# Three edge tables folded while the fourth comes, the diagonal's default written to memory, and TensorE loops in the first stage of a graph-attention layer

## The chip, the cores and the metric

The kernel runs on one core of a Trainium2 chip. Its time is the device time in microseconds (us) of one launch. Three runs of the kernel before gave 503.61, 492.89 and 503.67 us; the median is 503.61.

## The reference

384 nodes with 1024 features go through a layer norm, then two branches are added to them, then a second norm and an expert block. All matrices are fp32. Cut to what matters:

```python
xn = layernorm(x)                                   # (384, 1024)
q = xn @ wq.T + bq;  k = xn @ wk.T + bk;  v = xn @ wv.T + bv
q2, k2, v2 = heads(q @ wiq.T + biq), heads(k @ wik.T + bik), heads(v @ wiv.T + biv)   # 16 heads of 64
mask = full((384, 384), -inf)
mask = mask.at[src, dst].set(w[edge_type - 1])      # 12288 edges, the last of a pair counts
diag = diagonal(mask)                               # a missing diagonal becomes w[3]
mask = mask.at[i, i].set(where(isneginf(diag), w[3], diag))
attn = softmax(q2 @ k2.T * scale + mask)
x = x + (attn @ v2) @ wo.T + bo + mixer(xn)         # mixer: coeff = sum_d(fq * fk), coeff * v, @ Wo + bo
x = x + expert_ffn(layernorm(x))                    # one of 8 experts, chosen by a loss over the nodes
```

w is softplus of four edge weights. The mixer has three 1024x1024 projections and one back.

## The kernel before, in words

It is written by hand, engine by engine. Each engine's program is a fixed list, and semaphores order the lists among each other. Every 1024x1024 matrix comes in eight blocks of 128x1024, 512 KB each. A block is split in two parts of reduced precision: ScalarE writes the high part (line 554), VectorE the rest (line 927), and TensorE multiplies high by high, high by low and low by high. A `column_job` (line 1315) is that for one block: 24 matmuls of 384 columns, 16 at line 1321 and 8 at 1326. A `row_block` (line 1334) is 18 matmuls of 512 columns at line 1331.

**First stage.** 32 column jobs make q, k, v and q2 (jobs 0 to 7, 8 to 15, and so on). Weight slots and PSUM banks go round by four: job a uses slot `A_SLOTS[a % 4]` for the time a // 4 and bank `A_BANKS[a % 4]`. The fourth slot lies in tiles that are used later on: its raw weights in `mask`, its parts in `probT`; the profile shows these names for it. Jobs 0 to 23 read the normalised input xT, jobs 24 to 31 (q2) read q in T0. After them come v2 in eight row blocks, and between its halves the first k2 job.

**The edges beside it.** On VectorE each job also handles 3 of 96 columns of 128 edges: it compares keys (line 982) to find edges that a later one in the same column replaces, and writes addresses to `where` (line 989). GpSimd then scatters a column's weights to a table of 384x384 values in memory, one indirect DMA per column (line 470). Two edges of different columns can hit the same place, so scatters to one table must follow each other. There are four tables, each with a quarter of the edges and taken in turn 1, 2, 3, 0; a table's next scatter waits until its last one has landed. A later table's edges are to win. The tables begin as ABSENT (line 459). At the end GpSimd loads them to SBUF (line 479), table 0 to `mask`, the others to the three `later` regions of U.

**The mask on VectorE.** Its program has eight weight splits for the v2 stage; between the seventh and the last stands `default_diagonal`, behind the last `merge_table` three times. The diagonal is treated in table 0 alone: three comparisons (line 1007) and three predicated copies (line 1011). Each merge marks the present places of one table (line 1018) and copies them into the mask (line 1020).

**The pairs.** Then eight pairs of heads follow. Each has scores on TensorE (line 1447), six reads of scores plus mask on VectorE (line 1092), exponentials and normalising on ScalarE (lines 677, 684), a transposing trip of the probabilities through memory (VectorE 1108, SP's queue 383 and 391, ScalarE 665, VectorE 1073), the product with v2 (line 1459), and four column jobs: the next k2, and the mixer's q, k and v. The job of the mixer's q takes a PSUM bank that a score had, so TensorE waits in pair 0 until all six reads are done (`score_read`, line 1493).

Of the kernel before, what the change touches and what calls it, by code (L numbers as in the profile page):

```python
# [18 lines left out]
U32 = mybir.dt.uint32  # L19
ALU = mybir.AluOpType  # L20
# [4 lines left out]
P = 128  # L25
N = 384
D = 1024
NT = N // P
KB = D // P
# [6 lines left out]
STREAMS = 4  # L36
DEEP = CH // STREAMS
# [12 lines left out]
FIRST = 32  # L50
# [59 lines left out]
def gps_layer(nc, x, out, weights, conv, down, upT, up_b, down_b, conv_b, disc, bias_cols,  # L110
              rows, edge_weights, edge_rows, edge_cols, consts):
    with ExitStack() as ctx:
# [3 lines left out]
        def sem(name):  # L116
            return ctx.enter_context(nc.semaphore(name))
# [86 lines left out]
        row_bo = Q2[:].rearrange("p k n -> p (k n)")[:, 0:2 * D].rearrange("p (r d) -> p r d", r=2)  # L204
        k2f = U[:, NT * D:2 * NT * D]
        blank = Q2[:, 0:NT, :]
        bare = U[:, 4608:4608 + NT * P].rearrange("p (t n) -> p t n", t=NT)
        bias_rows = k2f[BIAS_ROW:BIAS_ROW + 2, 0:D]
        raw_down = k2f[:, D:D + KB * R].rearrange("p (k r) -> p k r", k=KB)
        raw_up = k2f[:, D + 512:D + 512 + KB * R].rearrange("p (k r) -> p k r", k=KB)  # L210
# [50 lines left out]
        where_ready = sem("where_ready")  # L261
        blanked = sem("blanked")
        first_mask_in = sem("first_mask_in")
        diag_step = sem("diag_step")
        scattered = [sem(f"scattered{g}") for g in range(STREAMS)]
        table_in = [sem(f"table_in{g}") for g in range(1, STREAMS)]
        mask_step = sem("mask_step")
# [171 lines left out]
        def _(pool):  # L439
# [22 lines left out]
            pool.wait_ge(key_calc, 1)  # L462
            pool.dma_start(key_dram, erow[:, 0:P]).then_inc(key_out, 16)

            for k in range(CH):

                g = QUARTERS[k % STREAMS]
                pool.wait_ge(where_ready, k // CJ + 3)
                pool.wait_ge(scattered[g], 16 * (k // STREAMS + 1))
                pool.indirect_dma_start(  # L470
                    tables[g], bass.IndirectOffsetOnAxis(ap=where[:, k:k + 1], axis=0),
                    evalue[:, k:k + 1], None, bounds_check=N * N - 1,
                    oob_is_err=False).then_inc(scattered[g], 16)
            for g, into in enumerate([mask[:]] + later):
                pool.wait_ge(scattered[g], 16 * (DEEP + 1))
                if g == 0:

                    pool.wait_ge(lo_ready[A_SLOTS[3]], FIRST // 4 + 1)
                pool.dma_start(into, tables[g].rearrange("(t p n) o -> p t (n o)", t=NT, p=P)).then_inc(
                    table_in[g - 1] if g else first_mask_in, 16)  # L480
# [361 lines left out]
        def _(dve):  # L842
# [156 lines left out]
                                             in1=dst[0][:, j, :].bitcast(F32), op0=ALU.add,  # L999
                                             op1=ALU.subtract).then_inc(bank_free[a % 4], 1)  # L1000

            def default_diagonal():

                dve.wait_ge(first_mask_in, 16)
                dve.wait_ge(id_in, 16)
                for t in range(NT):
                    dve.scalar_tensor_tensor(out=bare[:, t, :], in0=mask[:, t, t * P:(t + 1) * P], scalar=ABSENT,
                                             in1=ident, op0=ALU.is_equal, op1=ALU.mult).then_inc(diag_step, 1)
                dve.wait_ge(diag_step, NT)
                for t in range(NT):  # L1010
                    dve.copy_predicated(mask[:, t, t * P:(t + 1) * P], bare[:, t, :].bitcast(U32),
                                        ew[:, 3:4].broadcast_to([P, P])).then_inc(diag_step, 1)
                dve.wait_ge(diag_step, 2 * NT)

            def merge_table(g):

                dve.wait_ge(table_in[g], 16)
                dve.tensor_scalar(present, later[g], ABSENT, None, ALU.not_equal).then_inc(mask_step, 1)
                dve.wait_ge(mask_step, 2 * g + 1)
                dve.copy_predicated(mask[:].rearrange("p t n -> p (t n)"),  # L1020
                                    present.bitcast(U32).rearrange("p t n -> p (t n)"),
                                    later[g].rearrange("p t n -> p (t n)")).then_inc(mask_step, 1)
                dve.wait_ge(mask_step, 2 * g + 2)

            for a in range(FIRST):
                job(a)
# [24 lines left out]
            for r in range(9):  # L1051
                if r < 8:
                    split_weights(*slot_use(r + 2))
                if r == K2_FIRST:
                    q2_lo(0)
                if r == K2_FIRST + 1:
                    k2_lo(0)
                if r == 6:
                    default_diagonal()
            for g in range(STREAMS - 1):  # L1060
                merge_table(g)

            def pv_sum(j, h):
                r = slice(64 * h, 64 * h + 64)
# [240 lines left out]
        def _(pe):  # L1305
# [9 lines left out]
            def column_job(slot, use, src, bank):  # L1315

                o = PS[:, bank, 0:N]
                pe.wait_ge(hi_ready[slot], use + 1)
                for part in range(2):
                    for k in range(KB):  # L1320
                        pe.matmul(o, w_hi[slot][:, k * P:(k + 1) * P], src[part][:, k, :],  # L1321
                                  start=(k == 0 and part == 0), stop=False)
                pe.wait_ge(lo_ready[slot], use + 2)
                for k in range(KB):
                    wl = w_lo[slot][:, k * P:(k + 1) * P]
                    last = pe.matmul(o, wl, src[0][:, k, :], start=False, stop=(k == KB - 1))  # L1326
                last.then_inc(w_used[slot], 1)
# [80 lines left out]
            whole_part(1, w_hi, 1, False, False)  # L1408
            pe.wait_ge(lo_ready[A_SLOTS[1]], 2)
            whole_part(1, w_lo, 0, False, True).then_inc(w_used[A_SLOTS[1]], 1)  # L1410
            for a in range(2, FIRST):
                pe.wait_ge(bank_free[a % 4], a // 4 + 1)
                column_job(*A_USES[a], T0 if a >= 3 * KB else xT, A_BANKS[a % 4])

            for half in range(2):
                for kp in range(4):
# [246 lines left out]
```

## Time and profile before

| | |
|---|---|
| median of three runs | 503.61 us (492.89 to 503.67) |
| profiled execution, its own time | 478.61 us |
| its span, first to last instruction | 476.8 us |
| TensorE busy | 466.1 us, 98% |
| VectorE, ScalarE, GpSimd busy | 346.6, 258.5, 156.0 us |
| mean granted clock of TensorE | 0.993 |

The page of the profile gives these and the chain of work that ended last. By it 57% of the span is TensorE and 20% DMA; up to 195 us it runs through the scatters (15% and 7% for their DMAs and their issue), the mask's load and VectorE's merges, from there on through TensorE. A timeline row is: start, duration, engine, line, operation, output and input, how many, and in brackets the idle time before it with what ended it. Where neighbouring instructions are merged the duration is that of all of them.

### The profile page before, as it was taken

The numbers are of one execution on the slowest core, as the hardware profiler recorded it, in microseconds if no ns is written. First come the engines' busy times: TensorE is split into PE (matmuls) and PEld (weight loads), VectorE is DVE, ScalarE is ACT, GpSimd is POOL, SyncE is SP. The second block draws the span as 40 slices with busy tenths as digits, with TensorE's granted clock in tenths as the row PEclk, the third lists the DMA queues.
The fourth block names the chain that finished last, engine by engine and source line by source line (L and its number), as shares of the span: only waits on it lengthen the run. The fifth ranks groups of instructions, "written<-read, shape, count | busy, mean of one in ns | idle before, by whom it ended". The sixth has DMA issues, their size and how long they took to land.

```text
span 476.8 us, 7326 instructions
## 1 busy us (share of the span) xinstructions
PE 466.1 (98%) x2521; PEld 432.9 (91%) x2521; DVE 346.6 (73%) x796; ACT 258.5 (54%) x423; POOL 156.0 (33%) x176
## 2 busy tenths in 40 slices
PE   7999999999999999799999999999999999999996
PEld 5999999999999888699999999999998888888885
DVE  6968976677626237778889897898876994587394
ACT  3734533333324344668888788888875362163170
POOL 3136767767767762000210103022026000040200
PEclk9999999999999999799999999999999999999999
DMA  7876776566554446376676667577669854210463
GB/s 249 314 212 222 232 216 167 177 182 177 156 148 151 132 126 250 131 226 202 207 257 191 221 197 217 202 228 253 188 224 346 297 184 164 88 35 11 138 261 132
DMA packets 39049, 91.92 MB, mean 193 GB/s; under 512 B 7410, under 2 KB 20306, under 8 KB 38884
## 3 DMA queue, kind: packets, MB, share of 16 engines
q1 hardware_dynamic: 33604, 83.15, 54.2%
q0 software_dynamic: 4832, 7.45, 4.7%
q10 hardware_dynamic: 576, 0.85, 0.6%
q8 instruction: 20, 0.33, 0.3%
q14 instruction: 17, 0.14, 0.1%
HBM read 77.96 MB, written 13.47 MB: 192 GB/s over the span
## 4 chain that ended last, share of the span: by engine, by line
PE 57%; DMA 20%; issue 10%; POOL 7%; DVE 4%; POOLq 0%; ACT 0%; DVEq 0%; SPq 0%
PE PS L1331 21%; PE PS L1321 18%; DMA table<-evalue,where 15%; PE PS L1326 9%; POOL table L470 7%; PE PS L1459 4%; PE PS L1447 3%; PE PS L1583 2%; DMA mask<-table 1%; DMA U<-x 1%; DMA raw<-weights 1%; DMA key_dram<-V 1%; DMA U<-key_dram 1%; PE PS L1587 1%; DVE mask L1020 1%
## 5 line engine op out<-in xcount | busy, mean ns | idle before, releaser
L927 DVE TENSOR_TENSOR w_lo<-raw,w_hi 128x1024 fp32r<-128x1024 f32 x86 | 105.0, 1232 | 44.1 <-ACT w_hi L554 43.7
L554 ACT ACTIVATE w_hi<-raw 128x1024 fp32r<-128x1024 f32 x87 | 90.9, 1054 | 72.4 <-PE PS L1331 47.0
L470 POOL DMA_INDIRECT table<-evalue,where x96 | 104.4, 1087 | 48.0 <-issue 24.4
L1321 PE MATMUL PS<-xT_hi,w_hi 128*128 128x384 f32 x320 | 63.3, 339 | 3.3 <-DVE smax L1092 3.3
L1321 PE MATMUL PS<-xT_lo,w_hi 128*128 128x384 f32 x320 | 63.1, 339 | 0.0
L1326 PE MATMUL PS<-xT_hi,w_lo 128*128 128x384 f32 x320 | 62.0, 334 | 0.0
L1321 PEld LDWEIGHTS PS<-xT_hi,w_hi 128*128 128x128 f32 x320 | 57.1, 191 | 3.6 <-DVE smax L1092 3.6
L1321 PEld LDWEIGHTS PS<-xT_lo,w_hi 128*128 128x128 f32 x320 | 57.2, 191 | 0.0
L1326 PEld LDWEIGHTS PS<-xT_hi,w_lo 128*128 128x128 f32 x320 | 56.3, 188 | 0.0
L1331 PE MATMUL PS<-w_hi,T_hi 128*128 128x512 f32 x144 | 40.1, 391 | 0.0
L1331 PE MATMUL PS<-w_hi,T_lo 128*128 128x512 f32 x144 | 39.8, 389 | 0.0
L982 DVE SCALAR_TENSOR_TENSOR U<-U,V,cst 128x128 f32<-128x128 f32 x96 | 33.6, 350 | 8.0 <-DMA U<-key_dram 5.6
L1331 PE MATMUL PS<-w_lo,T_hi 128*128 128x512 f32 x144 | 37.8, 389 | 0.0
L616 ACT ACTIVATE T_hi<-PS,bias 128x384 fp32r<-128x384 f32 x24 | 13.8, 576 | 39.5 <-PE PS L1326 39.5
L502 POOL CAST vs<-V 128x384 fp32r<-128x384 f32 x8 | 5.0, 629 | 83.9 <-PE PS L1459 75.9
L1331 PEld LDWEIGHTS PS<-w_hi,T_lo 128*128 128x128 f32 x144 | 27.0, 188 | 5.7
L1331 PEld LDWEIGHTS PS<-w_lo,T_hi 128*128 128x128 f32 x144 | 27.0, 188 | 5.6
L1331 PEld LDWEIGHTS PS<-w_hi,T_hi 128*128 128x128 f32 x144 | 27.0, 188 | 5.2
L677 ACT ACTIVATE U<-U,nmax 128x384 f32<-128x384 f32 x48 | 28.9, 605 | 5.1 <-DVE nmax L1096 5.1
L1108 DVE STREAM_TRANSPOSE U<-U 128x384 f32<-128x384 f32 x48 | 24.1, 552 | 9.7 <-DMA turn<-U 9.7
L684 ACT ACTIVATE U<-U,rsum 128x384 f32<-128x384 f32 x48 | 25.8, 604 | 0.0
L997 DVE SCALAR_TENSOR_TENSOR T_lo<-PS,bias,T_hi 128x384 fp32r<-128x384 f32 x24 | 14.7, 615 | 14.9 <-ACT T_hi L616 14.9
(247 smaller groups left out, 810.9 us busy)
## 6 DMA issues: line engine op xcount, KB each, us to landing
raw<-weights SPq DMA_DIRECT2D x84, 512.0 KB, 4.5
turn<-U SPq DMA_DIRECT2D x16, 576.0 KB, 4.2
U<-turn SPq DMA_DIRECT2D x64, 144.0 KB, 2.9
U<-key_dram SPq DMA_DIRECT2D x32, 192.0 KB, 4.2
mask<-weights SPq DMA_DIRECT2D x9, 512.0 KB, 4.8
table<-Q POOLq DMA_DIRECT2D x4, 576.0 KB, 10.7
V<-conv SPq DMA_DIRECT2D x4, 512.0 KB, 5.3
U<-table POOLq DMA_DIRECT2D x3, 576.0 KB, 7.8
```

The source lines that it names most:

```text
L470: pool.indirect_dma_start(tables[g], bass.IndirectOffsetOnAxis(ap=where[:, k:k + 1], axis=0), evalue[:, k:k + 1], None, bounds_check=N * N ...
L554: act.activation(w_hi[slot][:], raw[slot][:], ACT.Copy).then_inc(hi_ready[slot], 1)
L677: act.activation(prob[:, h, t, :], prob[:, h, t, :], ACT.Exp, bias=nmax[:, h, t:t + 1], scale=SCALE, accum_out=ssum[:, h, t:t + 1]).then_i ...
L684: act.activation(prob[:, h, t, :], prob[:, h, t, :], ACT.Copy, scale=rsum[:, h, t:t + 1]).then_inc(prob_ready, 1)
L927: dve.tensor_tensor(w_lo[slot][:], raw[slot][:], w_hi[slot][:].bitcast(F32), ALU.subtract).then_inc(lo_ready[slot], 1)
L982: dve.scalar_tensor_tensor(out=key_junk, in0=key_row[:, s, c * P:(c + 1) * P], scalar=ekey[:, ch0 + c:ch0 + c + 1], in1=tri, op0=ALU.is_eq ...
L997: dve.scalar_tensor_tensor(out=dst[1][:, j, :], in0=PS[:, A_BANKS[a % 4], 0:N], scalar=bias[:, a:a + 1], in1=dst[0][:, j, :].bitcast(F32), ...
L1108: dve.transpose(blocks.rearrange("p (c m t i) -> p t m c i", c=NQ, m=NT, t=NT)[:, t], prob[:, h, t, :].rearrange("p (m c i) -> p m c i", m ...
L1321: pe.matmul(o, w_hi[slot][:, k * P:(k + 1) * P], src[part][:, k, :], start=(k == 0 and part == 0), stop=False)
L1326: last = pe.matmul(o, wl, src[0][:, k, :], start=False, stop=(k == KB - 1))
L1331: return pe.matmul(bank, src[part][:, 2 * kp + k2, t * P:(t + 1) * P], weights_in[slot][:, k2 * HALF:(k2 + 1) * HALF], start=start, stop=stop)
L1459: last = pe.matmul(PS[:, 7, 0:N], vs[:, m, h, :], probT[part][:, m, :], start=(m == 0 and part == 0), stop=(m == NT - 1 and part == 1))
```

## The change

Four edits. (1) A DMA on GpSimd's queue writes w[3] to the 384 diagonal places of table 0 in memory, after its blank and ahead of all scatters; an edge on the diagonal overwrites it. `default_diagonal` goes. (2) GpSimd loads the tables in the order 1, 2, 3, 0. (3) VectorE folds table 2 into table 1, then table 3, and copies the outcome into table 0's mask at the end. The first fold stands where the diagonal stood. (4) TensorE's jobs 4 to 31 become two loops over rounds of four jobs, five rounds that read xT and two that read T0; the waits take their values from a register.

```diff
+            pool.wait_ge(prep, 7)
+            pool.wait_ge(scattered[0], 16)
+            pool.dma_start(tables[0][::N + 1, :].rearrange("(t p) o -> p (t o)", p=P),
+                           ew[:, 3:4].broadcast_to([P, NT]), allow_slow_non_contiguous=True).then_inc(scattered[0], 16)
             for k in range(CH):
                 g = QUARTERS[k % STREAMS]
                 pool.wait_ge(where_ready, k // CJ + 3)
-                pool.wait_ge(scattered[g], 16 * (k // STREAMS + 1))
+                pool.wait_ge(scattered[g], 16 * (k // STREAMS + 1 + (g == 0)))
...
-            for g, into in enumerate([mask[:]] + later):
-                pool.wait_ge(scattered[g], 16 * (DEEP + 1))
+            for g, into in [(1, later[0]), (2, later[1]), (3, later[2]), (0, mask[:])]:
+                pool.wait_ge(scattered[g], 16 * (DEEP + 1 + (g == 0)))
...
-            def default_diagonal():
...
-            def merge_table(g):
-
+            def fold_table(g):
+
+                dve.wait_ge(table_in[0], 16)
                 dve.wait_ge(table_in[g], 16)
                 dve.tensor_scalar(present, later[g], ABSENT, None, ALU.not_equal).then_inc(mask_step, 1)
-                dve.wait_ge(mask_step, 2 * g + 1)
+                dve.wait_ge(mask_step, 2 * g - 1)
+                dve.copy_predicated(later[0].rearrange("p t n -> p (t n)"),
+                                    present.bitcast(U32).rearrange("p t n -> p (t n)"),
+                                    later[g].rearrange("p t n -> p (t n)")).then_inc(mask_step, 1)
+                dve.wait_ge(mask_step, 2 * g)
+
+            def merge_tables():
+
+                dve.tensor_scalar(present, later[0], ABSENT, None, ALU.not_equal).then_inc(mask_step, 1)
+                dve.wait_ge(first_mask_in, 16)
+                dve.wait_ge(mask_step, 5)
                 dve.copy_predicated(mask[:].rearrange("p t n -> p (t n)"),
                                     present.bitcast(U32).rearrange("p t n -> p (t n)"),
-                                    later[g].rearrange("p t n -> p (t n)")).then_inc(mask_step, 1)
+                                    later[0].rearrange("p t n -> p (t n)")).then_inc(mask_step, 1)
...
                 if r == 6:
-                    default_diagonal()
-            for g in range(STREAMS - 1):
-                merge_table(g)
+                    fold_table(1)
+            fold_table(2)
+            merge_tables()
...
-            for a in range(2, FIRST):
-                pe.wait_ge(bank_free[a % 4], a // 4 + 1)
-                column_job(*A_USES[a], T0 if a >= 3 * KB else xT, A_BANKS[a % 4])
+            for a in (2, 3):
+                pe.wait_ge(bank_free[a], 1)
+                column_job(*A_USES[a], xT, A_BANKS[a])
+
+            for src, begin, end in ((xT, 1, 3 * KB // 4), (T0, 3 * KB // 4, FIRST // 4)):
+                with pe.Fori(0, end - begin) as i:
+                    for s in range(4):
+                        pe.wait_ge(bank_free[s], i + (begin + 1))
+                        column_job(A_SLOTS[s], i + begin, src, A_BANKS[s])
```

VectorE between the last split of the v2 stage's first part and the first score read, before (w_lo is a weight split, U holds the tables and the marks):

```order
L927 TENSOR_TENSOR w_lo<-raw,w_hi 128x1024 [waits hi_ready2]
L1007 SCALAR_TENSOR_TENSOR U<-mask,cst 128x128 [waits id_in,first_mask_in]
L1007 SCALAR_TENSOR_TENSOR U<-mask,cst 128x128 x2
L1011 COPY_PREDICATED mask<-U,ew 128x128 [waits diag_step]
L1011 COPY_PREDICATED mask<-U,ew 128x128 x2
L927 TENSOR_TENSOR w_lo<-raw,w_hi 128x1024 [waits hi_ready0,diag_step]
L1018 TENSOR_SCALAR U<-U 128x1152 [waits table_in1]
L1020 COPY_PREDICATED mask<-U 128x1152 [waits mask_step]
L1018 TENSOR_SCALAR U<-U 128x1152 [waits table_in2,mask_step]
L1020 COPY_PREDICATED mask<-U 128x1152 [waits mask_step]
L1018 TENSOR_SCALAR U<-U 128x1152 [waits table_in3,mask_step]
L1020 COPY_PREDICATED mask<-U 128x1152 [waits mask_step]
```

and now, where `table_in1` to `table_in3` stand for tables 1 to 3 and `first_mask_in` for table 0:

```order
L930 TENSOR_TENSOR w_lo<-raw,w_hi 128x1024 [waits hi_ready2]
L1009 TENSOR_SCALAR U<-U 128x1152 [waits table_in2,table_in1]
L1011 COPY_PREDICATED U<-U 128x1152 [waits mask_step]
L930 TENSOR_TENSOR w_lo<-raw,w_hi 128x1024 [waits hi_ready0,mask_step]
L1009 TENSOR_SCALAR U<-U 128x1152 [waits table_in3,table_in1]
L1011 COPY_PREDICATED U<-U 128x1152 [waits mask_step]
L1018 TENSOR_SCALAR U<-U 128x1152 [waits mask_step]
L1021 COPY_PREDICATED mask<-U 128x1152 [waits mask_step,first_mask_in]
```

The wait for table 0 moved from ahead of all this work to the last instruction; six small instructions are gone.

TensorE at the start of the first loop, as it is now (before, the same rows without the first two and without the register step follow each other for all 28 jobs):

```order
L1417 UNCONDITIONAL_BRANCH
L1417 ISA
L1322 MATMUL PS<-xT_hi,w_hi 128x384 [waits hi_ready0,bank_free0]
L1322 MATMUL PS<-xT_hi,w_hi 128x384 x7
L1322 MATMUL PS<-xT_lo,w_hi 128x384 x8
L1324 REGISTER_ALU
L1327 MATMUL PS<-xT_hi,w_lo 128x384 [waits lo_ready0]
L1327 MATMUL PS<-xT_hi,w_lo 128x384 x7
```

and at its end:

```order
L1327 MATMUL PS<-xT_hi,probT_lo 128x384 x7
L1417 REGISTER_ALU
L1417 COMPARE_AND_BRANCH
L1417 UNCONDITIONAL_BRANCH
L1417 ISA
```

The matmuls and their waits are the same; a few control instructions came in per round.

## Rows read from the trace of the kernel before

**Rows 1.** The page: TensorE's busy time and instructions, matmuls and weight loads.
```profile
PE 466.1 (98%) x2521; PEld 432.9 (91%) x2521; DVE 346.6 (73%) x796; ACT 258.5 (54%) x423; POOL 156.0 (33%) x176
```
**Rows 2.** Waits of TensorE: who waited for whom, us, times, longest.
```profile
PE PS L1321 <- DVE smax L1092: 3.3, 1, 3.3
```
**Rows 3.** Timeline of TensorE around 195 us.
```profile
190.33 1.55 PE L1326 MATMUL PS<-T_hi,w_lo 128*128 128x384 f32 x8
195.20 2.93 PE L1321 MATMUL PS<-xT_hi,w_hi 128*128 128x384 f32 x8 [3.31 <-DVE smax L1092]
...
201.97 1.55 PE L1321 MATMUL PS<-xT_hi,w_hi 128*128 128x384 f32 x8
```
**Rows 4.** Windows: width, busy by engine, granted clock, DMA share, GB/s.
```profile
195.20:200.70 5.50, 5.50 (x17) 5.50 (x18) 4.93 (x10) 5.50 (x15) 0.00 (x0) 0.51 0.51 167
```
**Rows 5.** Timeline of GpSimd: last scatters and the table loads.
```profile
167.23 1.23 POOL L470 DMA_INDIRECT table<-evalue,where  x1 [0.30 <-DMA table<-evalue,where]
...
170.03 0.97 POOL L470 DMA_INDIRECT table<-evalue,where  x1 [0.30 <-issue]
171.31 1.33 POOL L470 DMA_INDIRECT table<-evalue,where  x1 [0.30 <-issue]
175.38 0.80 POOL L479 DMA_DIRECT2D mask<-table  x1 [2.74 <-DMA table<-evalue,where]
176.17 2.31 POOL L479 DMA_DIRECT2D U<-table  x3
```
**Rows 6.** DMA: busy tenths per us of 160 to 200; issues, median us to landing.
```profile
DMA  5900390039202830569999999880000000000597
...
table<-Q POOLq DMA_DIRECT2D x4, 576.0 KB, 10.7
U<-table POOLq DMA_DIRECT2D x3, 576.0 KB, 7.8
table<-evalue,where POOLq DMA_INDIRECT x96, 3.8
...
mask<-table POOLq DMA_DIRECT2D x1, 576.0 KB, 5.9
```
**Rows 7.** Timeline of VectorE from the last split to the merged mask.
```profile
174.69 1.23 DVE L927 TENSOR_TENSOR w_lo<-raw,w_hi 128x1024 fp32r<-128x1024 f32 x1 [2.37 <-ACT w_hi L554]
181.33 0.70 DVE L1007 SCALAR_TENSOR_TENSOR U<-mask,cst 128x128 f32<-128x128 f32 x3 [5.41 <-DMA mask<-table]
182.06 0.71 DVE L1011 COPY_PREDICATED mask<-U,ew 128x128 f32<-128x128 uint32 x3
...
183.94 0.75 DVE L1018 TENSOR_SCALAR U<-U 128x1152 f32<-128x1152 f32 x1
184.73 1.55 DVE L1020 COPY_PREDICATED mask<-U 128x1152 f32<-128x1152 uint32 x1
...
188.91 1.42 DVE L1018 TENSOR_SCALAR U<-U 128x1152 f32<-128x1152 f32 x1
190.37 1.55 DVE L1020 COPY_PREDICATED mask<-U 128x1152 f32<-128x1152 uint32 x1
```
**Rows 8.** Timelines of SP's queue and ScalarE: the first probability block comes back.
```profile
203.65 1.77 SPq L391 DMA_DIRECT2D U<-turn  x4
...
208.92 1.15 ACT L665 ACTIVATE probT_hi<-U 128x1152 fp32r<-128x1152 f32 x1
```
**Rows 9.** Timelines of GpSimd, VectorE and TensorE, up to 35 us.
```profile
10.71 3.04 POOL L459 DMA_DIRECT2D table<-Q  x4 [6.88 <-DMA raw<-weights]
...
34.70 0.97 POOL L470 DMA_INDIRECT table<-evalue,where  x1 [0.30 <-issue]
...
28.15 0.35 DVE L982 SCALAR_TENSOR_TENSOR U<-U,V,cst 128x128 f32<-128x128 f32 x1 [3.71 <-DMA U<-key_dram]
...
30.69 1.66 PE L1326 MATMUL PS<-xT_hi,probT_lo 128*128 128x384 f32 x8 [0.70 <-DVE probT_lo L927]
```
**Rows 10.** The page: TensorE's code queue (packets, MB, share of 16 engines).
```profile
q8 instruction: 20, 0.33, 0.3%
```

More of the change, by code:

```diff
@@ L206, in gps_layer @@
         blank = Q2[:, 0:NT, :]
-        bare = U[:, 4608:4608 + NT * P].rearrange("p (t n) -> p t n", t=NT)
         bias_rows = k2f[BIAS_ROW:BIAS_ROW + 2, 0:D]
@@ L263, in gps_layer @@
         first_mask_in = sem("first_mask_in")
-        diag_step = sem("diag_step")
         scattered = [sem(f"scattered{g}") for g in range(STREAMS)]
@@ L1000, in job @@
                                              op1=ALU.subtract).then_inc(bank_free[a % 4], 1)
-            def default_diagonal():
[L1004 to L1013, printed above, removed]
-            def merge_table(g):
+            def fold_table(g):
+                dve.wait_ge(table_in[0], 16)
                 dve.wait_ge(table_in[g], 16)
                 dve.tensor_scalar(present, later[g], ABSENT, None, ALU.not_equal).then_inc(mask_step, 1)
-                dve.wait_ge(mask_step, 2 * g + 1)
+                dve.wait_ge(mask_step, 2 * g - 1)
[7 more added lines that the diff above has]
+                dve.wait_ge(mask_step, 5)
                 dve.copy_predicated(mask[:].rearrange("p t n -> p (t n)"),
                                     present.bitcast(U32).rearrange("p t n -> p (t n)"),
-                                    later[g].rearrange("p t n -> p (t n)")).then_inc(mask_step, 1)
-                dve.wait_ge(mask_step, 2 * g + 2)
+                                    later[0].rearrange("p t n -> p (t n)")).then_inc(mask_step, 1)
+                dve.wait_ge(mask_step, 6)
             for a in range(FIRST):
```

## The prediction

> **What bounds the kernel now.** I read the engine totals first. TensorE is busy for 98% of the span, so only TensorE's own work and its few gaps can carry time [rows 1]. Next the waits of TensorE: the longest is 3.3 us for the last of six mask reads on VectorE (the softmax inputs of pair 0) [rows 2]. The timeline there shows the ending k2 job at 190.33 with 1.55 us, then nothing until 195.20 [rows 3]; the job ended at 190.33 + 1.55 = 191.9. The eight matmuls behind the gap take 2.93 us, later ones of the same shape 1.55. The granted clock says why: from 195.20 to 200.70 it is 0.51, which is 1.2 GHz of 2.4, after 3.3 us without matmuls [rows 4]. At half clock 5.5 us do the work of 2.75. So this place costs 3.3 + 2.7 = 6.0 us, and that is all the change can win here while TensorE has the rest of its work.
>
> Third, what ends that wait. It is a chain beside TensorE: the scatters, the table loads, then the merges on VectorE. The last four scatters (tables 1, 2, 3, 0) start between 167.23 and 171.31, the mask's load is issued at 175.38, the other three behind it [rows 5]. A scatter lands 3.8 us after its issue, the first load after 5.9, the other three after 7.8 as the median; the DMA share is near zero at 171 and again at 175 us and nine tenths from 178 on [rows 6]. VectorE has been free since 174.69 + 1.23 = 175.9 and waits 5.41 us for the mask; then 0.70 + 0.71 for the diagonal, 1.23 for a weight split, three comparisons and three predicated copies (1.55 the first, the third comparison 1.42), up to 191.9; then six reads, after which TensorE starts at 195.2, so 3.3 us for them [rows 3, 7].
>
> **The change, part by part.** *Table loads in the order 1, 2, 3, 0.* With 3.8 us to land, the last scatters of tables 1, 2 and 3 (167.23, one between, 170.03) are in at about 171.0, 172.5 and 173.8. GpSimd's queue issues its last scatter until 171.31 + 1.33 = 172.6. So the loads go out at 172.9, 173.7 and 174.5 (0.8 each, as now), and the mask's at 175.4 as now. The first two go to DMA engines that are nearly idle, so I take 5.9 us for table 2: in at 179.6. Table 3: 180.4 to 182.3 with 5.9 or 7.8. Table 0, now last, 7.8: 183.2 (5.9 would give 181.3).
>
> *VectorE.* Six diagonal instructions go, 0.70 + 0.71 = 1.4 us, which were on the chain. The large ones stay three comparisons and three copies, 0.75 + 1.55 = 2.3 a pair by the quickest. New order: fold of table 2 from 179.6 to 181.9; the weight split queued behind it to 183.1; fold of table 3 to 185.4; comparison to 186.2; copy into the mask to 187.8, for which table 0 (183.2) is in. The mask is ready at 187.8, not at 191.9: 4.1 us earlier. Bounds: loads 1.9 later and one comparison at 1.42 give 190.4 (1.5 us earlier); table 2 landing as fast as a scatter, in 3.8, gives 185.7 (6.2 earlier). Six reads in 3.3 us end at 191.1, and TensorE asks at 191.9. The wait goes, and with it the low clock: **-6.0 us**, less what the next parts cost. At the late bound 190.4 the reads end at 193.7, a wait of 1.8. The low clock set in somewhere in the 3.3 us gap; whether one of 1.8 would escape it is open. "TensorE: Matmul & The Clock Gate" of the Trainium skill, Part 1, says that the gate looks at times of its own, independent of the kernel. By that rule a short gap might meet the low clock or not from run to run, and this part would lie between -1.5 (dip kept) and -4.2 (dip gone) for this bound.
>
> *What is late next.* The pair's first probability block goes VectorE, memory, back, ScalarE, VectorE, TensorE. The reload is issued from 203.65 on, four pieces in 1.77 us, about 3 us to land, so in at 208; ScalarE takes it at 208.92 without waiting [rows 8]. TensorE's need moves 6.0 us earlier, the block only 4.1 (VectorE's reads): 1.9 us against 0.9 of slack. I charge 0.3, bounds 0 and 1.0. The later pairs show no TensorE wait.
>
> *The diagonal written to memory.* One DMA of 384 single elements on GpSimd's queue. It waits for VectorE's scaled edge weights, which come before any scatter's address, and for table 0's blank, the last of four issued by 13.75 and 10.7 us to land, thus about 24 us. Its issue is bounded by the 0.76 of a blank (also 384 rows), and it is out before the first address exists, which the key read of 28.15 has to precede. Table 0's first scatter comes at 34.70: more than the 10.7 us, the longest landing shown, so that scatter does not wait. What it can disturb: the key read that VectorE waits for until 28.15 (3.71 idle), and behind that the weight split that TensorE waits 0.70 for at 30.69 [rows 9]. A delay there reaches TensorE one for one. Below: nothing. Above: 3.8 us, the landing of a whole scatter. The elements equal three scatters, which elsewhere pass at 1.3 us each beside weight loads; spread over 16 engines they hardly occupy one. I charge 0.3. "DMA: Bandwidth & Descriptors" of the Trainium skill, in its closing tables, says that a strided last dimension becomes one descriptor per element; it gives no other sum here.
>
> *The loops.* Jobs 4 to 23 become five rounds and 24 to 31 two, 96 matmuls and their weight loads a round. The matmuls are the same. Added are a branch and a register step per round, five jumps back in all. TensorE works without a gap in this stage, and since the mask wait is gone, a bubble here would count fully. No row of this kernel shows a jump. Below: 0, since the sequencer may be ahead; above: if each jump had to fetch code anew, a page of code. The 20 pages of TensorE's code queue took 0.3% of 16 engines' span, 0.003 x 476.8 x 16 / 20 = 1.1 us each in transfer [rows 10], and a DMA as small as a scatter needs 3.8 to land: 5 x 3.8 = 19. Nearest is the case of a jump within code that is there: a round holds 192 matmuls and loads of some 5,042, or 0.76 of a page. I charge 0.3. "Advanced Engine Details and Errata" of the Trainium skill (Control Flow Timing) has about 108 ns for a compare-and-branch; five make 0.5 as an estimate by that page, and the sum would be 0.2 worse. The four fewer pages of code are worth nothing: 0.3% of the engines' time in all.
>
> *Sum.* -6.0 + 0.3 + 0.3 + 0.3 = -5.1. The profiled execution took 478.6 us (span 476.8 and 1.8 around it), so 473.5 in a profile. The median shown is 503.6, 25 us above it, and the three runs lie 10.8 apart. The trace doesn't contain these 25. If they lengthen the scatters, the mask wait is longer and 4 to 6 us still come off; if they are in TensorE, less comes off. I take the difference: 503.6 - 5.1 = **498.5 us**.
>
> **Rivals.** A measurement of this kernel tells 2%, about 10 us, from no change.
> (1) *Forecast*: wait and low clock go, 496 to 501. Chance 0.50.
> (2) *The mask is hardly the limit in unprofiled runs, or part of the wait and the low clock stay.* With the late bound and the dip kept, 478.6 - 1.5 + 0.9 is no change; so 501 to 505. For: 25 us unexplained. Against: the wait is the longest there is. Chance 0.22.
> (3) *The loops stall TensorE.* Place: the five jumps back. A jump refetches code, 3.8 us each, 19 in all; against -6.0 that is +13. If every gap also brings a dip of 2.7 as the one at 195, up to 5 x 2.7 = 13.5 more: 517 to 530. Break-even is 6.0 / 5 = 1.2 us a jump; slower by 2% needs 16 / 5 = 3.2. "Runtime: NRT & Kernel Launch" of the Trainium skill (Instruction fetch mechanics) states the rule: a jump to a target outside the two fetched pages stalls for a DMA, and full unrolling is preferred. For: a round of 0.76 page can begin in one page and end in the next. Against: the code came in by single pages spaced like the work without one gap in TensorE, so the sequencer is ahead, and what is queued covers a jump. Chance 0.08.
> (4) *The change comes out at a lower level than the median shown.* One of three runs took 492.9; with -5.1 that is 487.8. If a shorter chain makes such runs the rule, the gain passes 2%. For: 10.8 us between runs of one program is more than the whole place costs in the profile, so something else than the rows decides it, and a chain with slack would be less exposed. Against: nothing in the trace shows it. Chance 0.17.
> (5) A higher level unseen so far, 505 to 515, 0.03.
>
> The range takes (1), (2) and (4): **487 to 505**, leaving out (3), (5) and the ends. Faster by over 2% (below 493.5): (4) and a tail of (1), 0.22. Slower (above 513.7): (3) and part of (5), 0.10. Within: 0.68.
>
> **What would show it.** Loads of tables 1 to 3 issued from 172.9 on and the mask's last at 175.4; the last copy ending near 187.8; TensorE's wait for the mask read under 1 us, and no stretch of granted clock 0.5 near 195; TensorE's matmuls of jobs 4 to 31 without gaps. Wrong if gaps stand every 96 matmuls and more than 20 code pages arrive; if the first key read lands later than 28.1; or if the low clock comes all the same.

## The result: the change saves nothing that the median shows

In the first comparison, 22 launches (executions) of each kernel, the change has a median of **495.10 us** (491.45 to 503.33), the kernel before 494.74 (490.04 to 503.67): 0.1% apart. The comparison itself gives a ratio of 1.0186, 95% interval 1.0119 to 1.0253, which leaves open whether the change is slower by 2%; it goes by the launches within 1.5% of a kernel's fastest, but of these 16 and 14 launches the medians are 493.84 and 492.58, 0.3% apart, so I don't rest anything on it. The profiled launch of the change took 501.14 us. On four chips used later both kernels run some 20 us faster, and three comparisons there give the change 0.9988 [0.9950, 1.0026], 1.0013 [0.9977, 1.0049] and 0.9991 [0.9955, 1.0027] of before: no change. The forecast was 498.5. The measured 495.10 lies in the range of 487 to 505, but the gain of 5.1 did not come: the median of before had itself come down, from 503.61 over three launches to 494.74 over 22.

The page of the change's profile, first comparison (answers to [rows 1, 10]; PEclk is the granted clock in tenths, 40 slices of 12.5 us):

```profile
span 499.3 us, 7352 instructions
PE 476.3 (95%) x2521; PEld 435.3 (87%) x2521; DVE 343.5 (69%) x790; ACT 257.3 (52%) x423; POOL 153.4 (31%) x177
PEclk9999967997999899999999999999999999999999
q8 instruction: 16, 0.26, 0.2%
```

TensorE has the same 2521 matmuls, is busy for 10 us more than before and has 23 us outside its matmuls, against 10.7. The low clock is not near 195 us (slice 15 of 0 to 39) but in slices 5, 6, 9 and 13: about 62 to 87, 112 to 125 and 162 to 175 us. Four pages of code fewer arrive, as the shorter program has it.

Its waits of TensorE, the answer to [rows 2] (who waited for whom, us, times, longest):

```profile
PE PS L1322 <- issue: 9.2, 15, 1.4
PE PS L1327 <- issue: 5.6, 8, 1.3
PE PS L1369 <- DVE w_lo L886: 1.6, 1, 1.6
...
PE PS L1454 <- ACT U L751: 0.4, 1, 0.4
PE PS L1466 <- DVE probT_lo L1074: 0.2, 1, 0.2
```

The wait for the mask read is gone. In its place stand 14.8 us in 23 gaps put down to "issue": no engine and no transfer that the profile shows was waited for. The timeline of TensorE in the same launch shows how they look (start, duration, instruction, idle time before):

```profile
60.87 1.55 PE L1322 MATMUL PS<-xT_hi,probT_hi 128*128 128x384 f32 x8
62.25 1.47 PE L1322 MATMUL PS<-xT_lo,probT_hi 128*128 128x384 f32 x6
64.36 0.51 PE L1322 MATMUL PS<-xT_lo,probT_hi 128*128 128x384 f32 x2 [0.63 <-issue]
65.80 0.42 PE L1327 MATMUL PS<-xT_hi,probT_lo 128*128 128x384 f32 x1 [0.93 <-issue]
67.22 0.48 PE L1327 MATMUL PS<-xT_hi,probT_lo 128*128 128x384 f32 x1 [0.99 <-issue]
...
76.43 0.48 PE L1322 MATMUL PS<-xT_hi,w_hi 128*128 128x384 f32 x1 [1.41 <-issue]
77.13 2.20 PE L1322 MATMUL PS<-xT_hi,w_hi 128*128 128x384 f32 x5 [0.23 <-issue]
```

Eight matmuls in a row normally start 1.39 us apart from the next eight, 0.17 each. Here single ones start 0.7 or a multiple of it apart. Windows over the three stretches follow, then the first two of them in another launch of the change, the second of its three repeats below, where TensorE has no gap (width; busy by PE, PEld, DVE, ACT, POOL; granted clock; DMA share; GB/s):

```profile
60.00:80.00 20.00, 12.10 (x41) 9.01 (x41) 3.73 (x12) 2.98 (x5) 12.59 (x13) 0.67 0.24 66
...
110.00:125.00 15.00, 10.77 (x41) 8.72 (x40) 5.22 (x18) 4.53 (x6) 7.44 (x8) 0.77 0.23 75
...
150.00:166.00 16.00, 12.95 (x58) 10.69 (x58) 3.54 (x12) 3.63 (x5) 10.68 (x11) 0.89 0.09 25
```

```profile
60.00:80.00 20.00, 20.00 (x117) 20.00 (x116) 13.86 (x42) 7.66 (x10) 14.53 (x14) 1.00 0.69 190
...
110.00:125.00 15.00, 15.00 (x89) 15.00 (x88) 10.46 (x34) 5.47 (x8) 11.97 (x10) 1.00 0.64 189
```

117 matmuls in 20 us against 41. The low clock (1.2 of 2.4 GHz) came behind each stretch's first gaps, from 66.8 for 13.7 us, from 118.0 for 6.8 and from 162.3 for 3.4, 23.9 us in all. From job 0 to the first v2 column the launch takes 162.5 us where the profiled launch of before took 134.9, 27.6 more. Of these 14.8 are the gaps, and the other 12.8 are matmuls that took longer: in the 23.9 us TensorE is busy for 16.2, so the half clock accounts for 8.1 at most, and the rest are matmuls that stand alone, 0.33 to 0.5 us each where those in a row come 0.17 apart. The eight score pairs (first score to first output block) take 155.65 us against 160.48, and what stands behind them 130.6 both times. The gain in the pairs has the forecast's sign, but this launch can't show that it is the fold's: TensorE came 27 us late, and the mask, complete at 212.15, was ready 1.9 us before the first read of a score at 214.00.

### The profile page after: what moved, and what is told of

It reads as the page before. It is cut to its first block, busy times and chain, and to the rows that moved or that the text cites. A ratio compares the mean times of both kernels' runs of the same rounds, so it can differ in the third digit from the quotient of the medians.

```text
span 499.3 us, 7352 instructions
## 1 busy us (share of the span) xinstructions
PE 476.3 (95%) x2521; PEld 435.3 (87%) x2521; DVE 343.5 (69%) x790; ACT 257.3 (52%) x423; POOL 153.4 (31%) x177
## 4 chain that ended last, share of the span: by engine, by line
PE 89%; issue 3%; DVE 3%; DMA 3%; ACT 0%; SPq 0%; DVEq 0%
PE PS L1322 35%; PE PS L1332 26%; PE PS L1327 18%; PE PS L1466 4%; PE PS L1454 3%; PE PS L1590 1%; DMA U<-x 1%; DMA key_dram<-V 1%; PE PS L1310 1%; DMA U<-key_dram 1%; PE PS L1594 1%; DVE U L1298 1%; PE PS L1574 1%; DVE probT_lo L1074 0%; DVE stats L857 0%
## 5 line engine op out<-in xcount | busy, mean ns | idle before, releaser
L473 POOL DMA_INDIRECT table<-evalue,where x96 | 100.9, 1051 | 59.9 <-issue 29.7
L1322 PE MATMUL PS<-xT_hi,w_hi 128*128 128x384 f32 x320 | 65.2, 342 | 3.3 <-issue 3.2
L1327 PE MATMUL PS<-xT_hi,w_lo 128*128 128x384 f32 x320 | 63.5, 339 | 0.6 <-issue 0.6
```

Source lines behind the costliest of these rows:

```text
L473: pool.indirect_dma_start(tables[g], bass.IndirectOffsetOnAxis(ap=where[:, k:k + 1], axis=0), evalue[:, k:k + 1], None, bounds_check=N * N ...
```

## The experiments

On each of the four later chips the kernels ran interleaved with the kernel before. Times are medians with lowest and highest, then the number of launches, the ratio to before and its 95% interval. The expectations speak of theory A, that the loops starve TensorE of instructions, and theory B, that the slow stretches come to any kernel at random; from the delay experiment on also of theory C, that the end of the mask's chain and TensorE's need of it nearly coincide, so that a launch has the wait with its low clock or neither.

**The change and the kernel before again, elsewhere.** No edit.

> The whole change once more. Theory A: slow stretches again at the same places of the loops, 490 to 503 us. Theory B: slow stretches at other places, their number differing from launch to launch.

Measured: 474.95 (473.33 to 477.67, 12 launches), ratio 0.9988 [0.9950, 1.0026]. No slow stretch came, which neither theory had expected.

> The kernel before once more, for another profile of it. Theory A: TensorE has no idle time by issue, as in the profile shown, and the 490 to 503 us have another cause. Theory B: it has 10 to 20 us by issue, in stretches with steps of about 0.7 us, at places that don't repeat, and the span is 12 to 25 us above the 476.8 shown. Ratio 1.00 in both.

Measured: 474.18 (472.54 to 478.39, 12), ratio 1.0008 [0.9967, 1.0049]; its profiled launch, span 471.3, has no mask wait although nothing was edited. What differs from the first profile is one time stamp. Timelines of GpSimd and VectorE of this launch, answers to [rows 5, 7]:

```profile
169.88 0.97 POOL L470 DMA_INDIRECT table<-evalue,where  x1 [0.30 <-issue]
172.35 0.80 POOL L479 DMA_DIRECT2D mask<-table  x1 [1.50 <-DMA table<-evalue,where]
...
177.61 0.69 DVE L1007 SCALAR_TENSOR_TENSOR U<-mask,cst 128x128 f32<-128x128 f32 x3 [1.85 <-DMA mask<-table]
...
185.89 1.56 DVE L1020 COPY_PREDICATED mask<-U 128x1152 f32<-128x1152 uint32 x1
```

The mask's load goes out at 172.35, not 175.38, and the last copy ends at 187.45, not 191.92. Ninety-six scatters stand ahead of it. Their end moves by more than these 3 us: in six profiled launches with the old load order the mask's load goes out at 167.79, 171.46, 171.53, 172.35, 175.38 and 175.66. TensorE waits for the mask in the last two and in no other.

**The table edits alone, the loops alone.** The first is the change with TensorE's code of before, the second the kernel before with the change's loops. The edit of the first:

```
-            for a in (2, 3): ... (both Fori loops)
+            for a in range(2, FIRST):
+                pe.wait_ge(bank_free[a % 4], a // 4 + 1)
+                column_job(*A_USES[a], T0 if a >= 3 * KB else xT, A_BANKS[a % 4])
```

> The change without the loops: diagonal in memory, loads in the order 1, 2, 3, 0, the fold. Theory A: no slow stretch, no wait for the mask read, no low clock near 195 us, 472 to 475 us in the profile, ratio 0.985 to 0.99. Theory B: slow stretches as in before, TensorE late at the mask either way, so the fold wins little: ratio 0.99 to 1.00.

Measured: 473.33 (472.17 to 474.78, 12), ratio 0.9945 [0.9909, 0.9981], and no wait for the mask.

> The kernel before with TensorE's two loops and nothing else. Theory A (the loops starve TensorE of instructions, in stretches of 10 to 15 us in which matmuls come at steps of about 0.7 us): such stretches lie in jobs 4 to 31, TensorE's idle time by issue is 10 to 20 us, ratio to before 1.01 to 1.03. Theory B (the stretches come to any kernel at random, and the profile shown of before was a launch without one): ratio 0.995 to 1.005, since the loops cost nothing by themselves. Both: with a stretch in the first stage TensorE reaches the mask late and its wait there is gone.

Measured: 476.31 (474.29 to 479.84, 12), ratio 1.0011 [0.9974, 1.0048]. Its profiled launch has the mask wait and a low clock, and no gap in jobs 4 to 31: from job 4 to the first v2 column 116.5 us with loops (32.32 to 148.80), 116.5 without (before again, 32.03 to 148.51). Timeline of GpSimd and waits of TensorE:

```profile
175.66 0.81 POOL L479 DMA_DIRECT2D mask<-table  x1 [2.89 <-DMA table<-evalue,where]
```

```profile
PE PS L1321 <- DVE smax L1092: 2.9, 1, 2.9
```

The forecast's mechanism is there, the loops' stall is not.

**What the mask's lateness is worth.** In both orders four GpSimd fills of an unused tile (4.42 us in all) are put between the last scatter and the table loads. They wait until the last scatter has landed, so all four tables are complete when the first load goes out.

```
+            pool.wait_ge(scattered[QUARTERS[-1]], 16 * (DEEP + 1))   # + 2 in the new order
+            for n in range(4):
+                pool.memset(present, 0.0).then_inc(delayed, 1)
+                pool.wait_ge(delayed, n + 1)
             for g, into in ...
```

> The kernel before, with GpSimd filling an unused region four times (about 1 us each) between the last scatter and the table loads, so that the mask comes about 4 us later. Theory C (the mask chain and TensorE's 191.8 us arrive together, so a launch either has the wait with a low clock behind it or has neither): now every launch waits 4 to 8 us, with a low clock: 481 to 485 us, +7 to +11 over the lower half of the launches before, ratio about 1.015 to 1.02. Rival (the wait is not what separates the launches at 474 and at 479 us): the two groups stay, both up by 4 at most.

Measured, old order: 478.65 (477.75 to 480.27, 4), ratio 1.0100 [1.0040, 1.0161]. That is less than the 481 to 485 expected, but the two groups of times are gone as theory C has it: the mean granted clock of all four launches is 0.992 to 0.996.

> The same 4 us in the kernel with the change's table edits and without its loops. Theory C: the fold gives back 3 to 4 us here in every launch, so TensorE's wait is under 4 us, 477 to 481 us, 3 to 6 less than the kernel before with the same delay. Rival (the fold wins little since VectorE's work is the same): at most 2 less.

Measured, table edits: 480.80 (479.28 to 480.95, 4), ratio 1.0134 [1.0076, 1.0192]. I had expected the new order to be the faster one here, and it is the slower. Timelines of GpSimd, VectorE and TensorE, first old order, then new:

```profile
177.47 0.81 POOL L484 DMA_DIRECT2D mask<-table  x1 [0.30 <-POOL U L477]
...
182.18 0.69 DVE L1012 SCALAR_TENSOR_TENSOR U<-mask,cst 128x128 f32<-128x128 f32 x3 [5.74 <-DMA mask<-table]
...
191.20 1.54 DVE L1025 COPY_PREDICATED mask<-U 128x1152 f32<-128x1152 uint32 x1
...
196.03 2.44 PE L1326 MATMUL PS<-xT_hi,w_hi 128*128 128x384 f32 x8 [3.62 <-DVE smax L1097]
```

```profile
177.50 2.34 POOL L487 DMA_DIRECT2D U<-table  x3 [0.41 <-POOL U L480]
179.82 0.77 POOL L487 DMA_DIRECT2D mask<-table  x1
...
184.88 0.76 DVE L1014 TENSOR_SCALAR U<-U 128x1152 f32<-128x1152 f32 x1 [8.51 <-DMA U<-table]
...
192.59 1.43 DVE L1026 COPY_PREDICATED mask<-U 128x1152 f32<-128x1152 uint32 x1
...
197.31 2.93 PE L1327 MATMUL PS<-xT_hi,w_hi 128*128 128x384 f32 x8 [4.97 <-DVE smax L1098]
```

With all tables ready at the same time, the old order starts its diagonal on one landed table 4.7 us after the first load; the new one needs two and starts after 7.4. From there VectorE needs 9.1 us to the complete mask where the old order needs 10.6, so 1.4 of the 2.7 come back and 1.3 stay. So the folding order gains only when tables 1 to 3 are complete ahead of the last: what it buys is above all the earlier loads. TensorE's wait and half clock follow the mask's end (192.7: wait 3.6, 194.0: wait 5.0), so lateness of the mask does cost time; what is not there in most launches is the lateness.

**The diagonal's default alone.** The edge weights are written by DMA, VectorE's six instructions go, orders stay.

```
+            pool.dma_start(tables[0][::N + 1, :]..., ew[:, 3:4].broadcast_to([P, NT]), ...)
...
-                if r == 6:
-                    default_diagonal()
```

> The kernel before with the diagonal written to memory and without VectorE's six diagonal instructions; loads and merges in the old order. The mask comes 1.4 us earlier, which takes the wait of 3.3 to 1.9 in a late launch and away in an early one: ratio 0.996 to 1.000, fewer launches at 478 and more. If the 384 single elements delay the key read (VectorE's first comparison after 28.2 us, TensorE's wait at 30 us above 1.0): 0 to 1 us slower than before.

Measured: 475.72 (472.90 to 478.11, 10), ratio 1.0030 [0.9986, 1.0073], no gain; TensorE waits 0.6 for the low part behind the key read, before waits 0.58 and 0.70. The upper group of launches is still there, five of ten at 477.0 to 478.1, where before's own on this chip has a median of 478.9, which would fit 1.4 us less in late launches; ten launches are too few to show it. Its profiled launch is an early one. There the mask is complete 15.8 us after the first load, and 15.5 in the last profile of before: the weight split behind them waits for ScalarE and starts at 178.67 without them and at 178.70 with them, so they cost nothing there.

**Repeats, to tell the median's shift from chance.** The change, the table edits and before again:

> The whole change a third time. Theory B (slow stretches of TensorE's issue belong to the launch and the place, not to the kernel): none, 473 to 478 us, ratio 0.995 to 1.003, unless the kernel before is at 490 and more too. Theory A (the loops bring them): stretches in some launches, a spread to 490 us and more while the kernel before stays at 474.

Measured: 474.83 (473.76 to 476.74, 10), 1.0013 [0.9977, 1.0049].

> The kernel before, for a third profile of it. Theory B: where this place runs launches at 474 to 479 us, TensorE has no idle time by issue; where it runs them at 490 and more, it has 10 to 20 us of it in stretches with steps of 0.7 us, as the change had. Theory A: before never shows such a stretch, wherever it runs.

Measured: 473.84 (472.44 to 479.07, 10), 1.0001 [0.9945, 1.0058]. Timeline of GpSimd in its profiled launch, the earliest load of all:

```profile
167.79 0.80 POOL L479 DMA_DIRECT2D mask<-table  x1 [1.45 <-DMA table<-evalue,where]
```

> The table edits without the loops once more. Theory C: all launches between 472 and 475 us where before has two groups at 474 and 479: ratio 0.990 to 0.998. If the 1.5 us between its median and that of the whole change were chance, it is 474.5 or more here.

Measured: 473.58 (471.92 to 479.31, 10), 0.9960 [0.9911, 1.0009]. Seven of the ten launches lie between 471.9 and 474.5 as expected, the others at 475.77, 477.08 and 479.31.

> The kernel before, once more. Theory B: at a place with launches of 490 us and more its profile has TensorE idle by issue in steps of 0.7 us, 10 to 27 us in all; at a place with 474 to 479 none. Theory A: never.

Measured: 473.82 (472.35 to 478.30, 10), 0.9984 [0.9941, 1.0026].

> The whole change, beside it. Theory B: like the kernel before at the same place, within 1%. Theory A: 15 to 25 us more than before wherever stretches occur. At a quiet place both say 474 to 477 us, ratio 0.998 to 1.003.

Measured: 475.01 (472.79 to 476.51, 10), 0.9991 [0.9955, 1.0027].

**Other loops.** With the table edits, one loop of two rounds of eight jobs (jobs 4 to 19), the rest written out:

```
+            with pe.Fori(1, 5, 2) as i:
+                for s in range(8):
+                    pe.wait_ge(bank_free[s % 4], i + (1 + s // 4))
+                    column_job(A_SLOTS[s % 4], i + s // 4, xT, A_BANKS[s % 4])
```

> The change with one loop of two rounds of eight jobs (jobs 4 to 19, 384 matmuls and weight loads a round, 1.5 code pages) and the rest written out. If a jump over more than the pages at hand fetches code anew: one or two more packets in TensorE's code queue than its code needs, and a gap of 1 to 4 us at 100 us, if nothing that is queued covers it. If TensorE keeps more than two pages, or the queued matmuls cover the fetch: no gap, ratio 0.995 to 1.002 as for the change.

Measured: 472.66 (471.87 to 474.31, 10), 0.9947 [0.9908, 0.9985].

> The one loop of eight jobs once more, with one jump back instead of five. If jumps cost about 0.3 us each: 472 to 473.5 us again, 1.5 to 2 below the change. If the place decides instead, it moves with the tables-only kernel to within 0.5 us of it.

The same kernel on another chip: 472.69 (471.69 to 474.23, 10), 0.9958 [0.9919, 0.9997]. Its round is 1.5 pages of code by the instruction count. The page's code queue and TensorE's timeline around the jump back at 64.95, in the first of the two:

```profile
q8 instruction: 18, 0.29, 0.3%
```

```profile
63.57 1.55 PE L1327 MATMUL PS<-xT_hi,probT_lo 128*128 128x384 f32 x8
64.95 1.37 PE L1322 MATMUL PS<-xT_hi,w_hi 128*128 128x384 f32 x7
```

Eighteen packets, two fewer than before, and no gap (1.38 us from one eight to the next): no packet came beyond the program's own length, so what the jump goes back to was not fetched again. Then the change with only its first loop (jobs 4 to 23, four jumps) and only its second (24 to 31, one jump):

```
-            for src, begin, end in ((xT, 1, 3 * KB // 4), (T0, 3 * KB // 4, FIRST // 4)):
+            for src, begin, end in ((xT, 1, 3 * KB // 4),):
...
+            for a in range(24, FIRST):
+                pe.wait_ge(bank_free[a % 4], a // 4 + 1)
+                column_job(*A_USES[a], T0, A_BANKS[a % 4])
```

> The change with its first loop (five rounds of four jobs, four jumps back) and jobs 24 to 31 written out. If each jump costs about 0.3 us, or the first loop all of it: 1.2 to 1.5 over the table edits without loops (473.4), so 474.6 to 475. If the loops cost nothing by themselves: 473.0 to 473.8.

Measured: 473.67 (472.05 to 475.73, 10), 0.9950 [0.9910, 0.9991].

> The change with its second loop alone (two rounds, one jump back), jobs 4 to 23 written out. By jumps: 473.5 to 474. If it is the second loop that costs 1.5 us, which stands where the scatters are latest: 474.8 or more.

Measured: 473.44 (472.38 to 474.12, 10), 0.9949 [0.9910, 0.9988].

## Why the prediction was wrong, step by step

**The step that failed: "I take the difference: 503.6 - 5.1".** It takes the wait of the profiled launch for one that every launch has. Not every launch has it. Over the four chips there are 116 launches of before that ran beside the others, with their mean granted clock:

| kernel | launches | clock under 0.998 | their median | median of the others | mean of all |
|---|---|---|---|---|---|
| before | 116 | 41 | 478.56 | 473.64 | 475.54 |
| the change | 32 | 0 | | 474.83 | 474.95 |
| table edits, no loop | 22 | 1 | 479.31 | 473.37 | 473.71 |
| table edits, one of the two loops | 20 | 0 | | 473.57 | 473.61 |
| table edits, loop of eight jobs | 20 | 0 | | 472.66 | 472.83 |
| loops alone | 12 | 2 | 478.65 | 476.13 | 476.29 |
| the diagonal's default alone | 10 | 3 | 477.49 | 473.96 | 475.63 |

The 32 launches of before in the repeats above split alike, 8 and 24. The profile that I read is of the kind of the 41 (478.61, clock 0.993). In these the launch takes 478.56 - 473.64 = 4.9 us more, and no launch of the change is of that kind. In the other 75 the clock shows no loss; the profiled ones among such launches have the mask in time, so there is nothing to win, and the median launch is one of them. What is left there is what the change adds, 474.83 - 473.64 = 1.2 us. The median stays, and the mean falls by 0.6. The table edits without loops bring the mean down by 1.8, and 41 of 116 launches times 4.9 make 1.7. The delay experiment shows the same from the other side: with the loads held back by 4.4 us, all four launches of before lie at 478 to 480.

That 495.10 lies in the range is luck. The sum was laid on 503.61, the median of three launches, of which two are the slowest of the 22; the level of this place, 494.74, made up for the gain that is missing.

**-6.0 for the wait and the low clock: right for such a launch, a little large.** In the second repeat of the change the mask came as forecast. Timelines of GpSimd and VectorE:

```profile
171.54 1.32 POOL L473 DMA_INDIRECT table<-evalue,where  x1 [0.30 <-issue]
172.85 2.36 POOL L482 DMA_DIRECT2D U<-table  x3
175.80 0.76 POOL L482 DMA_DIRECT2D mask<-table  x1 [0.58 <-DMA table<-evalue,where]
...
179.87 0.76 DVE L1009 TENSOR_SCALAR U<-U 128x1152 f32<-128x1152 f32 x1 [3.73 <-DMA U<-table]
...
186.62 1.58 DVE L1021 COPY_PREDICATED mask<-U 128x1152 f32<-128x1152 uint32 x1
```

Loads from 172.85 (forecast 172.9), the mask's at 175.80 (175.4), first fold 179.87 (179.6), mask ready at 188.2 (187.8), TensorE without a wait at 191.94. The launch's pairs take 155.77 against 160.48, -4.7 where -6.0 + 0.3 was summed, and its span is 472.4 against 476.8, -4.4 against -5.1. In the two other repeats the loads began earlier still, at 169.77 and 169.19.

**+0.3 for what is late next: mis-sized.** Two of TensorE's waits in that launch:

```profile
PE PS L1454 <- ACT U L751: 0.6, 1, 0.6
PE PS L1466 <- DVE probT_lo L1074: 0.2, 1, 0.2
```

I named the probability block (0.2); the larger part, 0.6, is ScalarE's copy of the value bias (L751) that stands behind that block's split on ScalarE. Pair 1 lasts 21.8 us, 1.1 longer than in the profile of before, at my upper bound of 1.0; in the three profiled launches of before without the mask wait it lasts 21.0 to 21.2. It doesn't come in each launch: the launch of eight-job loops has neither wait.

**+0.3 for the diagonal: nothing.** In the first comparison, timelines of GpSimd, VectorE and TensorE, answers to [rows 9]:

```profile
24.23 0.77 POOL L465 DMA_DIRECT2D table<-ew  x1 [4.17 <-DMA table<-Q]
29.91 1.24 POOL L473 DMA_INDIRECT table<-evalue,where  x1 [4.91 <-DVE where L992]
...
27.70 0.35 DVE L985 SCALAR_TENSOR_TENSOR U<-U,V,cst 128x128 f32<-128x128 f32 x1 [3.46 <-DMA U<-key_dram]
...
30.24 1.67 PE L1327 MATMUL PS<-xT_hi,probT_lo 128*128 128x384 f32 x8 [0.45 <-DVE probT_lo L930]
```

Issued at 24.23 for 0.77 (forecast 24 and 0.76), and the key read is in at 27.7, not later than 28.15. In two repeats of the change it is in at 28.22 and 28.36, past the 28.1 that I had named as a sign of being wrong; but with loops alone, where nothing is written to the diagonal, it is in at 28.28, and in the old order with the delay at 28.68, so that sign tells nothing. The 1.4 us taken off for the six instructions of `default_diagonal` hold for loads as late as in the first profile; with early ones they are not on the chain, as the experiment with the diagonal alone shows.

**+0.3 for the loops: too small in the median, and not where the rival put it.** Both loops together stand at 474.83 against 473.37 without, 1.5 us, in launches without a low clock; the loops alone at 476.13 against 473.64, 2.5 us; and each of the three medians of the change (474.95, 474.83, 475.01) is above both of the table edits (473.33, 473.58). But four jumps alone give 473.67, one alone 473.44, and two rounds of eight jobs 472.66; so it is no price per jump, and no profile shows a gap in jobs 4 to 31 outside the first comparison: these jobs take 116.5 us in each of the 17 other profiles, with any loops or none. What differs between the launches without a mask wait lies in the pairs behind: 156.1, 155.8 and 156.7 us with the change, 154.6 and 154.7 with the loop of eight jobs, but also 156.8 and 155.9 with the table edits alone and 155.1, 156.4 and 154.7 before. A refetch would show as packets beyond the code's length; there are 16, 17, 18 and 19, what the loops' shorter programs leave of 20. "Runtime: NRT & Kernel Launch" of the Trainium skill (Instruction fetch mechanics) has a jump outside the two fetched pages wait for a DMA. With rounds of 0.76 and 1.5 pages no run here shows such a wait. What ties the 1.5 us to the loops stays open.

**The 25 us between profile and median: named as unexplained, and carried along.** The launch of 501.14 shows them as TensorE given its matmuls slowly in the first stage, with the low clock behind it. Whether the kernel before has the same stretches at that place is not shown: no profile of it was taken there. For the change the low clock there is the rule: the mean granted clock of its 22 launches is 0.967 to 0.986, which is 14 to 33 us at half clock in each, against 0.998 and more in all 32 of its launches elsewhere. For the 22 launches of before no clock is on record, but their times, 490 to 503.7, span the same as the change's, and none of the 17 other profiles, with or without loops, has a stretch. So I hold them for a matter of the place and not of the loops; that is argued, not shown.

What speaks for the loops is where the stretches lie. The jumps back are at 48.39, 72.93, 95.01, 111.65 and 153.12 us; the gaps of the second and third stretch begin 1.2 and 2.4 us behind a jump, 5 and 11 matmuls on, and the first stretch, from 63.7 to 77.1, runs across one, while the jumps at 48.39 and 95.01 have none. But rival (3) as I wrote it, gaps at each of the five jumps and more than 20 pages for code fetched anew, is not what came: 16 pages came, and none of them within the windows of the three stretches. A profile of before at that place would settle whether the loops have a part.

**Rival (2), "the mask is hardly the limit in unprofiled runs", was the right one**, at 0.22, in the mechanism though not in its 501 to 505, which stood on the median of three. What spoke for it was already in the table of times: launches of one program 10.8 us apart, and a profile outside them.

**A version that beats both** came out of the loop experiments: table edits with the one loop of eight jobs, 472.66 and 472.69, 0.5% and 0.4% under before in two comparisons, with intervals that end at 0.9985 and 0.9997; the change beside the first of them has 474.83. Both ratios are far under the 2% that a measurement tells, and the table edits without loops (473.33, 473.58) are close by.

## What to carry to other kernels

A wait read from one profile is worth its length only in launches that have it: when it ends a long chain of DMAs beside the bound engine, look at the chain's scatter over several launches, and at the mean granted clock of each, before taking it off a median. Reordering loads so that the last one is folded in late helps if the others finish earlier; when all are ready together it costs (1.3 us here), since two must land before the first step. When profile and median differ by more than the change can bring, the first thing to find out is what the other launches do.

## What the hardware did unexpectedly

- In the launch of 501.14 us TensorE got matmuls in steps of 0.7 us or multiples of it for 8 to 13 us at a time, three times, with no transfer or engine waited for, the scatters on GpSimd going on in their usual step (0.97 each) meanwhile. The DMA share was 0.09 to 0.24 in the windows around them; SP's queue issued no load between 64.9 and 81.1 us.
- After a wait for the mask the granted clock was half for 3.4 us where the wait was 2.9 (from 194.5 us) or 3.6 (from 196.6), and for 6.8 us where it was 3.3 (from 193.8, the launch of [rows 4]) or 5.0 (from 195.8). It set in within the gap in three of these, and 0.6 us behind the first matmul after it where the wait was 3.6. So the longer wait doesn't bring the longer low clock, and the same kind of gap brings a different loss: the low clock costs 1.7 us where matmuls run through all of 3.4 us, 2.7 in [rows 4].
- The same 96 scatters, four after four in the same order, finished up to 8 us apart between launches of the old load order, the first table's load going out between 167.79 and 175.66 us.
